# Unrolling the first attention of a two-layer kernel into one slot order, with output tiles spread over slots and the normalisation moved ahead of the maxima

## What is computed

```python
q_blhd = jnp.einsum('bld,dhk->blhk', x_bld, Wq)              # 16 heads of 64
latent_bll = jnp.einsum('bld,dc->blc', x_bld, Wkv_down)      # 64 wide
k_blhd = jnp.einsum('blc,chk->blhk', latent_bll, Wk_up)
v_blhd = jnp.einsum('blc,chk->blhk', latent_bll, Wv_up)
attn = jnp.einsum('bqhd,bkhd->bhqk', q_blhd, k_blhd) / 8     # causal
attn = softmax(where(mask, attn, min))
y_blhd = jnp.einsum('bhqk,bkhd->bqhd', attn, v_blhd)
x = layernorm(x + jnp.einsum('bqhd,hdo->bqo', y_blhd, Wout))
```

## Time and profile before

| | |
|---|---|
| median of 3 runs | 1884.75 us (1883.55 to 1886.87) |
| profiled execution, its time | 1887.51 us |
| its span in the profile | 1885.8 us |
| PE busy | 1670.2 us, 89% |
| DVE busy | 1211.7 us, 64% |
| ACT busy | 1017.6 us, 54% |
| POOL busy | 551.7 us, 29% |
| mean granted TensorE clock | 0.962 |

### The profile page before, as it was taken

The page is one execution under the profiler, slowest core; times in us unless marked ns, Lnnn a source line. Parts: engine busy times, 40 slices in busy tenths (PEclk is TensorE's granted clock), DMA queues, the critical chain, the costliest instruction groups (busy, mean ns, idle before and its releaser), DMA issues. The chain is left out here.

```text
span 1885.8 us, 32987 instructions
## 1 busy us (share of the span) xinstructions
PE 1670.2 (89%) x9124; PEld 1136.5 (60%) x9125; DVE 1211.7 (64%) x4166; ACT 1017.6 (54%) x2528; POOL 551.7 (29%) x683
## 2 busy tenths in 40 slices
PE   6899999999999989997869986799999998799996
PEld 4656665666666566654557754566656665457665
DVE  1886868687776868673744444688888877333345
ACT  1774756566674747472523344366666765653431
POOL 2001010010101010100154438888988873210001
PEclk9999999999999999998979998799999999999998
DMA  5211112021111111102034442978788777100000
GB/s 115 52 36 45 35 28 55 17 62 22 45 34 45 39 39 39 45 18 90 1 101 136 134 93 66 158 136 135 136 136 132 125 114 111 48 6 12 23 23 28
DMA packets 82750, 128.00 MB, mean 68 GB/s; under 512 B 14784, under 2 KB 40848, under 8 KB 82496
## 3 DMA queue, kind: packets, MB, share of 16 engines
q1 hardware_dynamic: 71232, 100.11, 26.0%
q0 software_dynamic: 9664, 25.93, 5.9%
q10 hardware_dynamic: 1728, 0.55, 0.2%
HBM read 73.59 MB, written 35.65 MB: 58 GB/s over the span
## 5 line engine op out<-in xcount | busy, mean ns | idle before, releaser
L136 ACT ACTIVATE c_probs<-c_probs,a_negmax 128x128 f32<-128x128 f32 (+3 forms) x512 | 279.7, 551 | 0.0
L1963 ACT ACTIVATE c_probs<-a_ps_st 128x384 f32<-128x384 f32 (+1 forms) x384 | 189.7, 526 | 130.6 <-PE a_ps_st L1763 127.9
L174 ACT ACTIVATE c_probs<-a_ps_trans 128x512 f32<-128x512 f32 (+1 forms) x256 | 124.8, 488 | 222.7 <-PE a_ps_trans L162 221.8
L126 DVE CUSTOM_DVE_ANT_0 c_probs<-a_ps_score,c_mask 128x128 f32<-128x128 f32 (+3 forms) x512 | 221.1, 487 | 35.2 <-PE a_ps_score L432 17.8
L2115 DVE CUSTOM_DVE_ANT_0 a_junk<-a_ps_score,c_mask 128x128 f32<-128x128 f32 (+3 forms) x512 | 220.7, 487 | 32.9 <-PE a_ps_score L1741 26.5
L615 POOL TENSOR_SCALAR a_rstd<-a_mv 128x4 f32<-128x4 f32 x8 | 1.8, 231 | 781.0 <-DVE a_mv L607 781.0
L162 PE MATMUL a_ps_trans<-c_ident,c_probs 128*128 128x128 f32 x1280 | 194.9, 284 | 39.4 <-DVE c_probs L146 25.6
L162 PEld LDWEIGHTS a_ps_trans<-c_ident,c_probs 128*128 128x128 f32 x1280 | 149.6, 144 | 112.2 <-issue 50.6
L431 PE MATMUL a_ps_score<-a_kh,a_qs 128*128 128x128 f32 (+3 forms) x512 | 168.4, 352 | 24.6 <-DVE a_negmax L126 16.4
L1597 POOL TENSOR_TENSOR a_ms<-a_ms,c_minus_half 128x16 f32<-128x16 f32 x64 | 187.6, 2934 | 0.1
L1763 PE MATMUL a_ps_st<-a_qs,a_ks 128*128 128x512 f32 (+3 forms) x512 | 155.2, 365 | 25.0 <-ACT c_probs L1963 15.0
(11 more groups left out here) (260 smaller groups left out, 3136.0 us busy)
## 6 DMA issues: line engine op xcount, KB each, us to landing
a_qs<-a_qlow SPq DMA_DIRECT2D x128, 128.0 KB, 2.2
bounce<-a_words SPq DMA_DIRECT2D x64, 256.0 KB, 2.0
a_qs<-bounce SPq DMA_DIRECT2D x128, 128.0 KB, 5.4
a_ks<-bounce SPq DMA_DIRECT2D x128, 128.0 KB, 5.9
slot_out<-m_y SPq DMA_DIRECT2D x80, 128.0 KB, 1.7
a_xT<-in_xT SPq DMA_DIRECT2D x8, 512.0 KB
a_xtok<-in_x SPq DMA_DIRECT2D x8, 512.0 KB
token_rows<-c_X SPq DMA_DIRECT2D x8, 512.0 KB, 5.7
```

Source lines behind the costliest of these rows:

```text
L126: dve.tensor_tensor_reduce(out=self.prob[:, h % 4, QOFF[i]:QOFF[i] + keys], in0=self.ps_score[g][:, at:at + keys], in1=self.C.mask[:, L - ...
L136: act.activation(at, at, ACT.Exp, scale=-1.0, bias=self.negmax[:, h % 4, i:i + 1], accum_out=self.rowsum[:, h % self.ring, i:i + 1]).then_ ...
L1963: act.activation(probT[:, r8, col:col + width], ps_st[item % 2][:, 0:width], ACT.Exp).then_inc(s_stc, 1)
```

## The change

The loop and the classes that served it go. The first attention becomes one list of slots `n` from 0 to 133, written out in full, with `n = 16 b + h`. Every slot holds one step of each kind: the last heads of a batch no longer share their slots with two heads of the next one. The projection of the next pair follows straight through the edge of a batch. The four output tiles of a batch stand behind slots 4, 6, 8 and 10 of the next one, and the additions at the head of slots 5, 7, 9 and 11. The last batch has its four tiles in one slot, in four banks. `latent` is in slot 12, `keys` in 13, `values` in slot 2, now in bank `ps_kv`, and `write` in slot 12. In VectorE's slot the order is now addition, normalise of n-2, mask_max of n, copy of n-3, q_low. `xT`, `kh`, `kl` and `latv` have two buffers each, `yT` has 12 parts in place of 8, and the tokens are loaded into `X` itself. The pass-through semaphore increments and the register arithmetic of the waits go.

```diff
-def over_batches(slot, eng, lag, ahead=1):
...
-    with eng.Fori(0, B - ahead) as b:
-        batch(b)
...
+BACK0 = 3
+NHEAD0 = B * H
+NPAIR0 = NHEAD0 // 2
+NY = 12
...
-        xT = S.sb("xT", [P, KT, L])
+        xT = [S.sb(f"xT{j}", [P, KT, L]) for j in range(2)]
...
+        kh = [S.sb(f"kh{j}", [P, L], R32) for j in range(2)]
+        kl = [S.sb(f"kl{j}", [P, L], R32) for j in range(2)]
+        latv = [S.sb(f"latv{j}", [P, TT, LD]) for j in range(2)]
...
-        NEXT, VALUES, OUT = H - 2, 4, {H + 4: (0, 1), H + 5: (2, 3)}
...
+        START, KEYS, VALUES, KEEP_VALUES, OUT, ADD, WRITE = 12, 13, 2, 3, (20, 22, 24, 26), (21, 23, 25, 27), 28
+        LOAD_X, LOAD_TOKENS = 2, 4
+        LAST_OUT, LAST_ADD = NHEAD0 + 4, NHEAD0 + 5
+        SLOTS_ALL = range(LAST_ADD + 1)
...
+        def batch_at(n, step):
+
+            b, left = divmod(n - step, H)
+            return b if left == 0 and 0 <= b < B else None
...
+        def out_tiles(n, steps, last):
+
+            if n == last:
+                return [(B - 1, t) for t in range(TT)]
+            return [(batch_at(n, steps[t]), t) for t in range(TT) if batch_at(n, steps[t]) in range(B - 1)]
+
+        def out_bank(b, t):
+
+            return [ps_kv, ps_q, ps_score[0], ps_score[1]][t] if b == B - 1 else ps_kv
+
+        def pair_ahead(n):
+
+            return n // 2 + 1 if n % 2 == 0 and n // 2 + 1 < NPAIR0 else None
+
+        def pair_behind(n):
+
+            return (n - 5) // 2 if n % 2 and 0 <= (n - 5) // 2 < NPAIR0 else None
...
-                with sp.Fori(0, B - 1) as b:
-                    low_words_and_tokens(b)
-                    load_x(b + 1)
-                    low_words(b + 1, 0)
...
+                low_words(0)
+                for n in SLOTS_ALL:
+                    if pair_ahead(n) is not None:
+                        low_words(pair_ahead(n))
+                    if batch_at(n, LOAD_X) is not None and batch_at(n, LOAD_X) + 1 < B:
+                        load_x(batch_at(n, LOAD_X) + 1)
+                    if batch_at(n, LOAD_TOKENS) is not None:
+                        load_tokens(batch_at(n, LOAD_TOKENS))
...
                 def out(b, t):
                     if t == 0:
-                        pe.wait_ge(s_yc, b * NPAIR + NPAIR + 1)
-                        if not (isinstance(b, int) and b == B - 1):
-                            pe.wait_ge(s_kl, b + 2)
+                        pe.wait_ge(s_yc, NPAIR * (b + 1))
+                        pe.wait_ge(s_latv, min(b + 2, B))
+                    if b < B - 1:
+                        if b or t:
+                            pe.wait_ge(s_sum, TT * b + t)
+                    elif t == 0:
+                        pe.wait_ge(s_sum, TT * b)
+                    elif t == 1:
+                        pe.wait_ge(s_qlo, 2 * NPAIR0)
                     else:
-                        pe.wait_ge(ln.s_sum, b * TT + t + 1)
+                        pe.wait_ge(s_max, TT * NHEAD0)
                     for p in range(NPAIR):
-                        last = pe.matmul(ps_kv[:, 0:D], yT[:, p, P * t:P * (t + 1)],
+                        last = pe.matmul(out_bank(b, t)[:, 0:D], yT[:, (NPAIR * b + p) % NY, P * t:P * (t + 1)],
                                          wvo[:, p, :], start=p == 0, stop=p == NPAIR - 1)
                     last.then_inc(s_out, 1)
...
+                latent(0)
+                project(0)
+                for n in SLOTS_ALL:
+                    if n < NHEAD0:
+                        scores(n)
+                    if 0 <= n - BACK0 < NHEAD0:
+                        transposes(n - BACK0, (0, 1))
+                    if batch_at(n, START) is not None and batch_at(n, START) + 1 < B:
+                        latent(batch_at(n, START) + 1)
+                    if pair_ahead(n) is not None:
+                        project(pair_ahead(n))
+                    if pair_behind(n) is not None:
+                        attend(pair_behind(n))
+                    if batch_at(n, VALUES) is not None:
+                        values(batch_at(n, VALUES))
+                    if 0 <= n - BACK0 < NHEAD0:
+                        transposes(n - BACK0, (2,))
+                    for b, t in out_tiles(n, OUT, LAST_OUT):
                         out(b, t)
...
-                    sm.vector_slot(dve, b, h)
...
-                    for t in OUT.get(h, ()):
-                        if t == 0:
-                            dve.wait_ge(s_xtok, b * 16 + 16)
-                        dve.wait_ge(s_out, b * TT + t + 1 + 1)
-                        ln.add(dve, b, t, ps_kv[:, 0:D], xtok[:, t, :])
-                    if h == H + 6:
-                        ln.write(dve, b)
...
+                def add(b, t):
+                    if t == 0:
+                        dve.wait_ge(s_xtok, 16 * (b + 1))
+                        if b >= 1:
+                            dve.wait_ge(s_x, TT * b)
+                    dve.wait_ge(s_out, TT * b + t + 1)
+                    at = X[:, b * TT + t, :]
+                    dve.tensor_tensor(at, out_bank(b, t)[:, 0:D], at, ALU.add).then_inc(s_sum, 1)
+                    dve.wait_ge(s_sum, TT * b + t + 1)
+                    dve.bn_stats(stats[:, t, :], at).then_inc(s_stat, 1)
+                    dve.wait_ge(s_stat, TT * b + t + 1)
+                    dve.bn_aggr(mv[:, t, :], stats[:, t, :]).then_inc(s_mv, 1)
...
+                for n in SLOTS_ALL:
+                    for b, t in out_tiles(n, ADD, LAST_ADD):
+                        add(b, t)
+                    if 0 <= n - 2 < NHEAD0:
+                        normalise(n - 2)
+                    if n < NHEAD0:
+                        mask_max(n)
+                    if 0 <= n - BACK0 < NHEAD0:
+                        copy_turned(n - BACK0, 1)
+                    if pair_ahead(n) is not None:
+                        q_low(pair_ahead(n))
+                    if batch_at(n, KEYS) is not None and batch_at(n, KEYS) + 1 < B:
+                        keys(batch_at(n, KEYS) + 1)
+                    if batch_at(n, WRITE) is not None and batch_at(n, WRITE) < B - 1:
+                        write(batch_at(n, WRITE))
+                write(B - 1)
 
```

More of the change, by code:

```diff
@@ L72, in sem @@
         return self.sems[-1]
-def start_at_one(eng, *sems):
-    for s in sems:
-        eng.sem_inc(s, 1)
 def due(value):
     return not isinstance(value, int) or value > 0
[L86 to L209, removed]
@@ L212, in over_batches @@
-def over_batches(slot, eng, lag, ahead=1):
[L217 to L228, removed]
-    with eng.Fori(0, B - ahead) as b:
-        batch(b)
-    for b in range(B - ahead, B - 1):
-        batch(b)
-    for h in range(lag, H + lag):
-        slot(B - 1, h)
+BACK0 = 3
@@ L434, in attend, with scores @@
-                def attend(b, p):
-                    sm.need_probT(pe, b * H + 2 * p + 1)
-                    pe.wait_ge(s_yc, b * NPAIR + p + 1)
-                    if p == 0:
-                        pe.wait_ge(s_latv, b + 1)
+                def scores(n):
+                    b, g, c = n // H, n // 2, n % 2
+                    pe.wait_ge(s_qhi, n + 1)
+                    pe.wait_ge(s_qdma[g % 2][c], 16 * (g // 2 + 1))
+                    if n % H == 0:
+                        pe.wait_ge(s_kl, b + 1)
+                    for grp, tiles in enumerate(SGROUP):
+                        if n >= 1:
+                            pe.wait_ge(s_max, TT * (n - 1) + tiles[-1] + 1)
+                        for i in tiles:
+                            keys = P * (i + 1)
+                            to = ps_score[grp][:, SCOL[i]:SCOL[i] + keys]
+                            q = qs[:, g % 2, c, P * i:P * (i + 1)]
+                            pe.matmul(to, q, kh[b % 2][:, 0:keys], start=True, stop=False)
+                            last = pe.matmul(to, q, kl[b % 2][:, 0:keys], start=False, stop=True)
+                        last.then_inc(s_score, 1)
@@ L571, in _, with mask_max @@
-                keys(0)
-                q_low(0, 0)
-                start_at_one(dve, ln.s_sum, ln.s_x, sm.s_pt_dve)
-                over_batches(slot, dve, LAG)
+                def mask_max(n):
+                    for grp, tiles in enumerate(SGROUP):
+                        dve.wait_ge(s_score, n * 3 + grp + 1)
+                        for i in tiles:
+                            keys = P * (i + 1)
+                            dve.tensor_tensor_reduce(
+                                out=prob[:, n % 4, QOFF[i]:QOFF[i] + keys],
+                                in0=ps_score[grp][:, SCOL[i]:SCOL[i] + keys], in1=C.mask[:, L - keys:L], scale=-1.0,
+                                scalar=3.0e38, op0=ALU.add, op1=ALU.min,
+                                accum_out=negmax[:, n % 4, i:i + 1]).then_inc(s_max, 1)
@@ L675, in keep @@
             act.activation(self.xs[j][:, k, :], self.ps[k][:], ACT.Copy).then_inc(self.s_xs, 1)
-def in_twos(eng, n, step):
-    step(0, 0)
-    step(1, 1)
-    with eng.Fori(1, n // 2) as r:
-        for j in range(2):
```

(1 more changed line is left out.)

302 lines of the change are left out of this document (140 added, 162 removed).

## The result

| kernel | median of 4 runs | lowest to highest |
|---|---|---|
| before | 1885.81 us | 1883.55 to 1887.58 |
| changed | 1813.49 us | 1810.03 to 1816.37 |

The ratio is 0.962 (95% interval 0.9595 to 0.9637): 72 us less, where 71.8 were forecast. The profiled execution of the changed kernel took 1810.03 us, 77.5 less than that of before.

A forecast was written before the change was run, and what follows sets the result against it. TensorE was taken as the bound. Gains of 60 us in six middle batches, 4 in the first stretch and 7 in the last make 71, from the median 1884.75 to 1813.7; forecast 1813, range 1798 to 1838.

The forecast's parts named there:

- The loop's edge: At the jump back, VectorE's unexplained 2.22 us stall goes: about 2.3 us per batch, and the clock's drop loses its first cause.
- The 18.5 us go: On VectorE, normalising n-2 ahead of the maxima of n removes TensorE's 18.5 us of waits for late normalised heads.
- The tight point: Odd head's maxima end just as the next head's last score bank wants them: 0.15 us per pair, 0.6 per batch.
- rival B: VectorE becomes the bound because `q_low` keeps its 1.1 us wait: cycle 9.85 against 9.2, gain 48, time 1837; chance 0.17.
- The pairs with a tile: Slot pairs with an output tile last 12.6 us on TensorE against 8.75 + 1.1 on VectorE, which catches up there.
- The tiles: Output tiles spread, each after an even slot, find the bank free: the 6.7 us of waits for it go.
- The new pinch: Slots 12 and 13 gain token writes, low keys and latent: about 1.2 us of waiting at the scores of slot 14.
- One step of each kind per slot: A projection or an `attend` in every slot covers ScalarE's copy of a transposed group: the 10.5 us of waits go.
- C: The edge's 2.3 us are not the jump's and stay in straight code: gain 46 to 56, about 1834; chance 0.08.
- D: Slower: straight code must be fetched without end and engines stall; one stall per two slots would give 1967; chance 0.03.
- E: Even better: no pinch and no tight point, all 1.8 us per batch go: gain 84, time 1801; chance 0.17.

The follow-up runs named there:

- e1: Kernel before, with its two loops written out and the same order on every engine: 1851.7 us, ratio 0.985 to the kernel before.
- e10: Changed kernel with the normalisation back behind the copy and the output tiles two by two: 1822.2 us, ratio 0.972 to the kernel before.
- e3: Changed kernel with the normalisation back behind the copy and ahead of `q_low`: 1799.6 us, ratio 0.958 to the kernel before.
- e2: Kernel before, loops kept, with the normalisation of head n-2 ahead of the maxima of head n: 1886.1 us, ratio 1.004 to the kernel before.
- e4: Changed kernel with the four output tiles two by two behind slots 4 and 5, additions ending those slots: 1834.7 us, ratio 0.977 to the kernel before.
- e8: Changed kernel with the token writes moved from slot 12 to slot 4 of the next batch: 1794.5 us, ratio 0.957 to the kernel before.
- e9: Changed kernel with the token writes at slot 4 and the normalisation back behind the copy: 1789.6 us, ratio 0.954 to the kernel before.
- e6: Changed kernel with `q_low` of an even slot moved behind the next slot's normalisation: 1826.9 us, ratio 0.966 to the kernel before.

## Why the prediction came out, step by step

The time was right to 1 us (1813.5 against 1813), and so close by luck: of the steps below it two were sized at half or less, one was wrong, and their errors cancelled. Where the losses lay (the loop's edge, the output tiles, the copy) was right. The steps from before to after, each between two neighbouring kernels of the table, per batch:

| step | forecast | measured | between |
|---|---|---|---|
| no jump | 2.3, and 1.7 of the clock | 3.55 | before and e1 |
| one step of each kind per slot, and all other moves | 1.75 (10.5 / 6) | 3.8 | e1 and e10 |
| tiles spread | 1.1 (6.7 / 6) | 3.7 | e10 and e3 |
| normalisation ahead | 3.1 (18.5 / 6), less the new waits | -0.6 | e3 and changed |
| together | 10.0 (102.6 to 92.6) | 10.4 | |

The forecasts of the rows make 9.95 before the new waits. The prediction also took off 0.3 more of the waits for maxima and 1.5 for ends of matmuls exposed ahead of waits ((18.9 - 10) / 6), and put on 1.8 of new waits, which leaves its 10.0.

- **The loop's edge** was right in place and cause. Its size in the sum was 2.3 plus the 1.7 of the clock; 3.55 was measured, and 4.1 in the batches of e1 without a drop of the clock.
- **"The 18.5 us go"** is the step that was wrong, as a credit to the order on VectorE. The waits by that name do go, but in each of four comparisons with the rest held equal the order costs: 1.1 (e2 and before), 1.0 (e4 and e10), 0.6 (changed and e3), 0.7 (e8 and e9). What freed VectorE took most of these waits away without the order: spreading the tiles (14.7 us in e10 to 10.7 in e3) and moving the writes (3.3 in e9). I read late normalised heads as a symptom of VectorE being late as a whole. The price that the prediction named was maxima 1.4 us later and `q_low` without its cover (its waits are 69.4 us for 54.0 in e3). The order as a whole costs more than it gains; how that splits between the two, no run shows.
- **The tight point** was mis-sized. I took 0.15 per pair without a tile, on 9.19. The pair lasts 9.65, over the 9.4 that I had named as the mark of a wrong prediction. In the layout a late maximum had no consequence beyond its own wait. In the rows the last bank of scores comes late, so the projection starts 494.37 - 491.78 = 2.59 us into the slot in place of 2.31, and `q_low` 5.91 (497.69) in place of 5.5. That this makes the next maxima late in turn, and so closes a loop, is argued from these rows; no run cut that loop alone. e6 bears it out: where `q_low` hardly waits, the pairs behind slots 12, 14 and 0 take 8.90, 9.88 (0.47 of it a wait for the transfer) and 9.17 us, for 10.66, 9.65 and 9.67 in the changed kernel. In such pairs VectorE's cycle sets the pace (8.75 of work, 0.73 of `q_low`'s wait, the rest gaps), so rival B had the mechanism of two pairs in eight right, and of the pinch's (9.85 forecast, 9.65 measured), and its total wrong.
- **The pairs with a tile** were over-priced: 12.35 measured, 9.19 + 3.37 = 12.56 taken. If a tile adds its whole 3.37 there, a pair of pure work is 8.98 us, and a batch 8 x 8.98 + 4 x 3.37 + 3.77 = 89.1 in place of 90.8. The 9.19 of the earlier trace rows would then have 0.2 us of hidden waiting in it, though no bracket stood there; the 8.90 of e6 speaks for it. This error and that of the tight point have opposite signs: over a batch the pairs with a tile came out 1.0 below the forecast and those without 0.6 above.
- **The tiles** gave 3.7 where 1.1 stood in the sum. "VectorE catches up there" was written down and not priced.
- **The new pinch** was right: 1.16 us at the scores of slot 14 in each batch, 1.2 forecast, and shown by e8.
- **One step of each kind per slot** took the 10.5 us of waits for the copy away: no such row is left in e10 or after. Of the other 2 us of the 3.8, 0.6 are the two drops of the clock that e1 still had (2 x 1.7 / 6) and e10 (clock 1.00) has not. The rest was not taken apart: e10 also differs from e1 in the places of the values, the latent and the token writes, and in its double buffers. TensorE's busy time is 8.8 lower in e10 (545.89 for 554.66), of which 3.2 are the drops (93.5 against 91.9 in a batch of e1); where the rest comes from, no run tells.
- **Rivals** C and D fell with e1 and the changed kernel: in the middle batches of the latter TensorE, VectorE and ScalarE show no "issue" wait at all. E, no waits at all, is nearly what e8 does, at 90.9 and not 90.8.

## What to carry to other kernels

This is what one kernel showed. When an engine off the path is late as a whole, moving one late result ahead on it may only rename the wait; look for the slots in which it has spare time (here those with an output tile) and move its extra work there, or spread what gives it that time. Price a slot from a place where both engines have slack, since a stretch called busy can hold waits without a bracket. And a producer of a transfer is due when the transfer must start, not when its result is read.

## What the runs showed that I had not expected

- Busy time of TensorE held waiting: 563.7 us over six batches before, 554.7 without the jump, 545.9 in e10, 538.6 in e3 and 537.2 in e9, with the same matmuls. Only a part of that is the clock (0.98 before, 0.99 in e1, 1.00 in the others). The Trainium skill ("Perfetto Trace Analysis", summary of the profiler window per engine type) says that a matmul's end in the profile is estimated; the trace agrees, as a matmul starts on the maxima's end with no idle time shown.
- The kernel with more idle time on its bounding engine was the faster: e3 has 10.7 us of named waits and 91.6 per batch, the changed kernel 7.2 and 92.2.
- Writing the loops out cost nothing that a trace shows: the first instruction queue grew from 45 packets and 0.74 MB to 71 and 1.16, and VectorE's "issue" waits in the middle batches are gone.
